# Scores and maxima of a tiled attention issued as four column tiles of 32 instead of one whole-array matmul

## Chip, cores and metric

One core of a Trainium2 chip runs the whole program. The metric is the device time of one execution in microseconds (us); of several runs the median is taken.

## What is computed

Sixteen images of 64 channels and 56 x 56 = 3136 pixels go through two layers. The first is attention inside windows of 7 x 7 pixels, with cosine scores, a bias table, three group norms and an MLP of width 256. The second is full attention over all 3136 pixels of an image, with 4 heads of 16 channels. Cut to what matters:

```python
# layer 1, of the layer-0 output x (n = 3136, heads = 4, d = 16)
qkv = jnp.einsum('oc,bchw->bohw', w_qkv, x)
q, k, v = jnp.split(qkv.reshape(b, 3 * c, n), 3, axis=1)
attn = jax.nn.softmax(jnp.einsum('bhdn,bhdm->bhnm', q, k) * scale, axis=-1)
out = jnp.einsum('bhnm,bhdm->bhdn', attn, v).reshape(b, c, h, w)
return jnp.einsum('oc,bchw->bohw', w_proj, out) + x
```

## The kernel before, in words

**Tiles of the second layer.** The keys and queries of a head lie in `k_stack` and `q_stack` in bf16, as six products' worth of three-piece splits stacked on 96 partitions (STACK), and three more rows (SHIFT) that subtract each query's maximum. The 3136 tokens are 25 tiles of 128 (TILES) on one side and 8 groups of 392 (GTOK) on the other. A stage is half of the queries (4 groups of 392) of one head, so an image has 8 stages and 8 x 25 = 200 quads. For each quad, that is for one tile of 128 keys:

- four steps `score` (function `score`, line 1285; matmul on line 1293): 99 rows, 128 keys as weights, 392 queries moving, out to one of three PSUM banks (SCORE_BANKS). Unit u first waits until the exponential of unit u - 3 is done.
- four exponentials on ScalarE (line 881), from PSUM to a ring of eight buffers in SBUF (`exps`, EXP_RING), in f32.
- one step `weigh` (line 1296; matmul on line 1304): four matmuls of `v_all` (128 rows, 32 columns, f32) with the four exponentials moving. Matmul j writes the PSUM partitions 32 j to 32 j + 31 of one bank, so the four lie side by side in the array as column tiles. An f32 matmul shows in the trace as two MATMULs and two LDWEIGHTS, so one `weigh` is eight of each.

The maxima are made ahead of a stage: a step `max` (line 1159) has two matmuls, 96 rows, 128 queries as weights, 392 keys moving, to the two banks of a slot, and VectorE reduces 784 columns to one (line 945). With 4 heads, 25 tiles and 4 pairs of groups there are 400 steps `max` per image, two per quad.

**Slots.** All steps of the first layer, the maxima, the shifts and the final projection use two PSUM slots in turn (RING_BANKS, banks 5 and 6, and 3 and 4). A step waits (function `free`) until the step two before it in the slots has been emptied by VectorE or ScalarE.

**Order.** The order of each engine's steps is written out by a planner when the program is built, with a fixed cost of each step and a fixed cost for going between steps that it lists as tiled and the others. The change leaves the planner's costs and lists alone, so every engine has its steps in the same order before and after. Image b + 1's first layer is woven into image b's attention. The first-layer steps on TensorE, per image: `qk` 4 (line 1173), `sum` 1 (line 1182, column tiles of 32), `spread` 4 (line 1190), `wscore` 16 (line 1200), `wval` 8 (line 1208), `wtrans` 16 (line 1218), `wpv` 8 (line 1229, column tiles of 32), `wproj` 8 (line 1236), `gn` 6 (line 1241), `mlp1` and `mlp2` 8 each (lines 1248, 1256), `gqk` 4 (line 1264), `gv` 3 (line 1273), and of the second layer `shift` 8 (line 1166) and `final` 4 (line 1282).

Of the kernel before, what the change touches and what calls it, by code (L numbers as in the profile page):

```python
# [10 lines left out]
GTOK = TOKENS // GROUPS  # L11
# [8 lines left out]
STACK = PIECES * D1  # L20
SHIFT = 3
# [5 lines left out]
SCORE_BANKS = 3  # L27
# [374 lines left out]
def attention_mlp_kernel(nc, x, qkv0, qkv0_b, logit_scale, table, rel_index, proj0, proj0_b, gn1_w, gn1_b,  # L402
# [10 lines left out]
    with ctx:  # L413
        def sb(name, shape, dt=f32):
            return ctx.enter_context(nc.sbuf_tensor(name, shape, dt))

        def sem(name):
            return ctx.enter_context(nc.semaphore(name))
# [42 lines left out]
        q_stack = sb("q_stack", [128, H1, PADTOK], bf16)  # L461
        k_stack = sb("k_stack", [128, H1, PADTOK], bf16)
# [20 lines left out]
        PS = ctx.enter_context(nc.psum_tensor("PS", [128, 8, 512], f32))  # L483
# [25 lines left out]
        s_scores, s_exps, s_pv_done, s_out_copied, s_out_stored = (sem(n) for n in (  # L509
            "scores", "exps", "pv_done", "out_copied", "out_stored"))  # L510
# [609 lines left out]
        def _(pe):  # L1120
            mm = nc.tensor.matmul
# [4 lines left out]
            for c in range(7):  # L1126
# [3 lines left out]
                   stop=True).then_inc(s_bias_product, 1)  # L1130
# [8 lines left out]
            def step(it, b, before):  # L1139
# [7 lines left out]

                if it.kind == "score":
                    score(it.i, b)
                elif it.kind == "weigh":  # L1150
                    weigh(it.i, b)
                elif it.kind == "max":
                    stage, tile, pair_ = it.i, it.j, it.k
# [2 lines left out]
                    free()  # L1156
                    for j in range(2):
                        chunk = 2 * pair_ + j
                        last = mm(PS[:, it.bank + j, 0:GTOK], q_stack[0:STACK, stage // 2, tile * 128:(tile + 1) * 128],  # L1159
                                  k_stack[0:STACK, stage // 2, chunk * GTOK:(chunk + 1) * GTOK], start=True, stop=True)  # L1160
                    last.then_inc(s_max_filled, 1)
                elif it.kind == "shift":
                    t0, t1 = STAGE_TILES[it.i % 2]
# [4 lines left out]
                elif it.kind == "qk":  # L1168
                    pe.wait_ge(s_x_by_windows, t * 8 + 2 * it.i + 2)
                    free()  # L1170
                    for j in range(2):
                        g = 2 * it.i + j
                        last = mm(PS[:, it.bank + j, 0:GTOK], w_qk0[:], x_w[:, g * GTOK:(g + 1) * GTOK],
                                  start=True, stop=True)
                    last.then_inc(s_qk_product, 1)
                elif it.kind == "sum":
                    pe.wait_ge(s_qk_squares, t * 4 + 4)
                    free()
                    for r in range(2):
                        for j in range(4):  # L1180
                            g = 4 * r + j
                            last = mm(PS[32 * j:32 * j + 32, it.bank, 0:GTOK], w_head_sum[:, r, :],
                                      tok_h[:, g * GTOK:(g + 1) * GTOK], start=(r == 0), stop=(r == 1))
                    last.then_inc(s_head_sums, 1)
                elif it.kind == "spread":
                    pe.wait_ge(s_norms_inverted, t + 1)
                    free()
                    for j in range(2):
                        g = 2 * it.i + j
                        last = mm(PS[:, it.bank + j, 0:GTOK], w_spread[:, g // 4, g % 4, :], tok_h[:, 0:GTOK],  # L1190
                                  start=True, stop=True)
                    last.then_inc(s_norms_spread, 1)
                elif it.kind == "wscore":
# [3 lines left out]
                    for i in range(4):  # L1197
                        w = 4 * half + i
                        q0, m = g * GTOK + w * WTOK, (64, WTOK)[w == 7]
                        last = mm(PS[64 * (w % 2):64 * (w % 2) + m, it.bank + i // 2, 0:GTOK],  # L1200
                                  tok_unit[0:CH + WTOK, q0:q0 + m], kmask[0:CH + WTOK, :, w * WTOK:(w + 1) * WTOK],
                                  start=True, stop=True)
                    last.then_inc(s_win_scores, 1)
                elif it.kind == "wval":
                    pe.wait_ge(s_x_twice, t * 8 + it.i + 1)
                    free()
                    for w in range(8):
                        last = mm(PS[0:2 * WTOK, it.bank, w * CH:(w + 1) * CH],  # L1208
                                  x_tw[:, w, :, :].rearrange("c a m -> c (a m)"), w_v0[:], start=True, stop=True)
                    last.then_inc(s_win_v, 1)  # L1210
                elif it.kind == "wtrans":
# [3 lines left out]
                    for p in range(2):  # L1215
                        for q in range(4):
                            c0 = (2 * half + p) * GTOK + q * 2 * WTOK
                            last = nc.tensor.transpose(PS[0:2 * WTOK, it.bank + p, q * 128:(q + 1) * 128],  # L1218
                                                       win_scores[:, c0:c0 + 2 * WTOK], ident_f32[:])
                    last.then_inc(s_win_transposed, 1)  # L1220
                elif it.kind == "wpv":
# [4 lines left out]
                    for w in range(8):  # L1226
                        for q in range(4):
                            c0 = q * 128 + 64 * (w % 2)
                            last = mm(PS[32 * q:32 * q + 32, it.bank, w * WTOK:(w + 1) * WTOK], win_v[:, w, q, :],
                                      win_probs_t[0:2 * WTOK, w // 2, c0:c0 + WTOK], start=True, stop=True)  # L1230
# [12 lines left out]
                elif it.kind == "mlp1":  # L1243
                    c = it.i
                    pe.wait_ge(s_mlp_in, t * 4 + c // 2 + 1)
                    free()
                    for e in range(2):
                        last = mm(PS[:, it.bank + e, 0:GTOK], w_1[:, 128 * e:128 * e + 128],  # L1248
                                  tok_qk[0:CH, c * GTOK:(c + 1) * GTOK], start=True, stop=True)
                    last.then_inc(s_mlp1, 1)  # L1250
                elif it.kind == "mlp2":
                    c = it.i
                    pe.wait_ge(s_hidden, t * 16 + 2 * c + 2)
                    free()
                    for e in range(2):
                        last = mm(PS[0:CH, it.bank, 0:GTOK], w_2[:, e, :], hidden[:, 2 * (c % 2) + e, :],  # L1256
                                  start=(e == 0), stop=(e == 1))
                    last.then_inc(s_mlp2, 1)
                elif it.kind == "gqk":
                    pe.wait_ge(s_z_ready, t * 4 + it.i + 1)  # L1260
                    free()
                    for j in range(2):
                        g = 2 * it.i + j
                        last = mm(PS[:, it.bank + j, 0:GTOK], w_qk1[:], z_w[:, g * GTOK:(g + 1) * GTOK],
                                  start=True, stop=True)
                    last.then_inc(s_gqk, 1)
                elif it.kind == "gv":
# [3 lines left out]
                    for tile in range(t0, t1):  # L1271
                        n_ = tile - t0
                        last = mm(PS[:, it.bank + n_ // 8, (n_ % 8) * CH:(n_ % 8 + 1) * CH],  # L1273
                                  z_w[:, tile * 128:(tile + 1) * 128], w_v1[:], start=True, stop=True)
                    last.then_inc(s_gv, 1)
                elif it.kind == "final":
# [3 lines left out]
                    for j in range(2):  # L1280
                        sl = slice((2 * k + j) * GTOK, (2 * k + j + 1) * GTOK)
                        last = mm(PS[0:CH, it.bank + j, 0:GTOK], w_p1[:], att[:, sl], start=True, stop=True)  # L1282
                    last.then_inc(s_final_proj, 1)

            def score(u, b):
                quad, j = u // 4, u % 4
                stage, kt = quad // TILES, quad % TILES
                h, c = stage // 2, 4 * (stage % 2) + j
                if kt == 0 and j == 0:
                    pe.wait_ge(s_shift_loaded, (b * STAGES + stage) * 48 + 48)  # L1290
                if u >= SCORE_BANKS:
                    pe.wait_ge(s_exps, b * UNITS + u - SCORE_BANKS + 1)
                mm(PS[:, u % SCORE_BANKS, 0:GTOK], k_stack[0:STACK + SHIFT, h, kt * 128:(kt + 1) * 128],  # L1293
                   q_stack[0:STACK + SHIFT, h, c * GTOK:(c + 1) * GTOK], start=True, stop=True).then_inc(s_scores, 1)

            def weigh(quad, b):
                stage, kt = quad // TILES, quad % TILES
# [14 lines left out]
            for it in PROLOGUE["PE"]:  # L1312
                step(it, -1, before)
            with pe.Fori(0, IMAGES - 1) as b:
                before = lead_in_emptied(b)
                for it in MORE["PE"]:
                    step(it, b, before)
            before = lead_in_emptied(IMAGES - 1)
            for it in LAST["PE"]:
                step(it, IMAGES - 1, before)  # L1320
# [57 lines left out]
```

## Time and profile before

| what | value |
|---|---|
| median of 3 runs | 10134.87 us |
| lowest and highest | 10125.32 and 10156.81 us |
| the profiled execution's own time | 10121.69 us |
| its span, first to last instruction | 10119.9 us |
| PE (matmuls) busy | 9685.7 us, 96% |
| VectorE busy | 7762.6 us, 77% |
| ScalarE busy | 6507.8 us, 64% |
| GpSimd busy | 974.3 us, 10% |
| mean granted TensorE clock | 0.968 of full speed |

PE stands for TensorE's matmuls and PEld for its weight loads. The busy time of PE takes each matmul from its start to the end of its latency, so matmuls that overlap are joined; how fast TensorE really goes is read from the distance between starts.

### The profile page before, as it was taken

How to read it: one execution, taken by the hardware profiler on the slowest of the kernel's cores; microseconds unless marked ns; L12 is line 12 of the kernel's file. 1: busy time of each engine (PE TensorE's matmuls, PEld its weight loads, DVE VectorE, ACT ScalarE, POOL GpSimd, SP SyncE). 2: the span in 40 equal slices, each digit the busy share in tenths (PEclk: the TensorE clock that was granted, in tenths of full speed). 3: DMA queues.
4: the chain of work that ended last, by engine and by line, in shares of the span. 5: the costliest groups of instructions: out<-in, count | busy, mean ns of one | idle time of the engine just before them, and what ended most of it. 6: DMA issues, size and time to landing. Idle time of an engine off the chain costs nothing.

```text
span 10119.9 us, 221389 instructions
## 1 busy us (share of the span) xinstructions
PE 9685.7 (96%) x69254; PEld 3807.6 (38%) x69254; DVE 7762.6 (77%) x10052; ACT 6507.8 (64%) x14066; POOL 974.3 (10%) x834
## 2 busy tenths in 40 slices
PE   5899999999999999999999999999999999999998
PEld 2333333333333343333433333333333433333332
DVE  4787777878778787787877778777787877878785
ACT  1466666666666667666666666666666666666676
POOL 3100101010010110101101010010101101011000
PEclk8799999999999999999999999999999999999999
DMA  0202011020110201102011020201102011020100
GB/s 24 35 7 39 10 21 27 6 41 8 22 26 5 42 8 27 21 8 40 7 29 20 9 39 7 37 13 21 27 6 41 9 24 24 5 43 8 25 16 16
DMA packets 109028, 213.92 MB, mean 21 GB/s; under 512 B 52854, under 2 KB 84534, under 8 KB 107706
## 3 DMA queue, kind: packets, MB, share of 16 engines
q1 hardware_dynamic: 107842, 198.78, 12.2%
q8 instruction: 663, 10.86, 0.5%
q14 instruction: 523, 4.28, 0.1%
HBM read 66.03 MB, written 41.47 MB: 11 GB/s over the span
## 4 chain that ended last, share of the span: by engine, by line
PE 83%; DVE 5%; DMA 4%; SPq 3%; issue 2%; ACT 2%; POOL 1%; DVEq 0%; ACTq 0%; POOLq 0%
PE PS L1304 23%; PE PS L1293 21%; PE PS L1159 20%; PE PS L1200 3%; DVE small L945 3%; PE PS L1218 2%; DMA x_in<-in_x 2%; PE PS L1208 2%; PE PS L1248 2%; PE PS L1256 2%; SPq L677 2%; ACT exps L881 1%; PE PS L1282 1%; PE PS L1273 1%; PE PS L1236 1%
## 5 line engine op out<-in xcount | busy, mean ns | idle before, releaser
L881 ACT ACTIVATE exps<-PS 128x392 f32<-128x392 f32 x12800 | 5591.0, 499 | 3029.7 <-PE PS L1293 2919.7
L945 DVE TENSOR_REDUCE small<-PS 128x1 f32<-128x784 f32 x6400 | 5942.3, 967 | 1172.7 <-PE PS L1159 1126.8
L1293 PE MATMUL PS<-q_stack,k_stack 99*128 99x392 bf16 x12800 | 3524.3, 336 | 31.8 <-ACT exps L881 19.3
L1159 PE MATMUL PS<-k_stack,q_stack 96*128 96x392 bf16 x12800 | 3186.0, 338 | 150.8 <-DVE small L945 79.6
L1304 PE MATMUL PS<-exps,v_all 128*32 128x392 f32 x25600 | 2823.2, 513 | 19.4 <-ACT exps L881 13.2
L1293 PEld LDWEIGHTS PS<-q_stack,k_stack 99*128 99x128 bf16 x12800 | 1200.0, 98 | 2418.8 <-ACT exps L881 1566.3
L1159 PEld LDWEIGHTS PS<-k_stack,q_stack 96*128 96x128 bf16 x12800 | 1049.3, 99 | 1728.4 <-DVE small L945 894.1
L1304 PEld LDWEIGHTS PS<-exps,v_all 128*32 128x32 f32 x25600 | 507.5, 108 | 998.5 <-issue 603.0
L780 POOL TENSOR_TENSOR win_scores<-win_scores,small 128x784 f32<-128x784 f32 x256 | 383.8, 1500 | 3351.2 <-DVE small L995 3351.2
L1200 PE MATMUL PS<-kmask,tok_unit 113*64 113x392 f32 (+1 forms) x2048 | 391.5, 506 | 7.5 <-DMA tok_unit<-in_query_ident 7.5
L983 DVE TENSOR_REDUCE small<-PS 128x16 f32<-128x784 f32 x256 | 249.2, 973 | 129.3 <-PE PS L1200 124.8
L838 ACT ACTIVATE win_probs_t<-PS 98x1024 f32<-98x1024 f32 x256 | 262.0, 1024 | 98.0 <-PE PS L1218 96.9
L1218 PE MATMUL PS<-ident_f,win_scores 128*98 128x128 f32 x2048 | 277.0, 280 | 18.7 <-DVE small L945 10.7
L986 DVE TENSOR_TENSOR win_scores<-PS,small 128x784 f32<-128x784 f32 x256 | 249.4, 974 | 31.5
L833 ACT ACTIVATE win_scores<-win_scores 128x784 f32<-128x784 f32 x256 | 221.0, 863 | 63.0 <-DVE win_scores L986 62.7
L793 POOL TENSOR_TENSOR att<-att,inv_sums 64x784 f32<-64x784 f32 x66 | 120.9, 1850 | 1459.0 <-DMA inv_sums<-scratch_rden 1459.0
L994 DVE TENSOR_REDUCE small<-win_scores 128x16 f32<-128x784 f32 x256 | 246.1, 961 | 14.1 <-ACT win_scores L833 10.9
L1218 PEld LDWEIGHTS PS<-ident_f,win_scores 128*98 128x98 f32 x2048 | 231.4, 130 | 66.3 <-DVE small L945 42.3
L1040 DVE SCALAR_TENSOR_TENSOR tok_h<-PS,vec,tok_h 64x392 f32<-64x392 f32 x128 | 79.1, 618 | 212.6 <-PE PS L1256 209.2
L1208 PE MATMUL PS<-w_v,x_tw 64*98 64x64 f32 x2048 | 210.6, 255 | 8.0 <-DVE win_scores L986 8.0
L930 DVE BATCH_NORM_STATS2 small<-tok_h 64x6 f32<-64x392 f32 x384 | 208.4, 556 | 9.8 <-ACT tok_h L848 1.1
L1208 PEld LDWEIGHTS PS<-w_v,x_tw 64*98 64x98 f32 x2048 | 192.9, 167 | 49.5 <-DVE win_scores L986 33.4
(102 smaller groups left out, 3938.5 us busy)
## 6 DMA issues: line engine op xcount, KB each, us to landing
q_stack<-tok_qk SPq DMA_DIRECT2D x320, 98.0 KB, 3.5
k_stack<-tok_qk SPq DMA_DIRECT2D x320, 98.0 KB, 4.2
kmask<-tok_unit SPq DMA_DIRECT2D x1024, 12.2 KB
scratch_att<-o_st SPq DMA_DIRECT2D x512, 26.0 KB
att<-scratch_att SPq DMA_DIRECT2D x33, 392.0 KB
z_half<-scratch_z SPq DMA_DIRECT2D x33, 392.0 KB, 11.1
inv_sums<-scratch_rden SPq DMA_DIRECT2D x132, 98.0 KB, 3.3
out<-inv_sums SPq DMA_DIRECT2D x33, 392.0 KB, 3.7
```

Source lines behind the costliest of these rows:

```text
L780: nc.gpsimd.tensor_tensor(S3, S3, rden[:, 16 * half:16 * half + 16].unsqueeze(2) .broadcast_to([128, 16, WTOK]), ALU.mult).then_inc(s_win_ ...
L838: nc.scalar.activation(win_probs_t[0:2 * WTOK, 2 * half:2 * half + 2, :], PS[0:2 * WTOK, it.bank:it.bank + 2, :], ACT.Copy)\
L881: nc.scalar.activation(exps(u), PS[:, u % SCORE_BANKS, 0:GTOK], ACT.Exp, scale=D1 ** -0.5).then_inc(s_exps, 1)
L945: nc.vector.tensor_reduce(max_parts[:, n_:n_ + 1], slot(), op=ALU.max, axis=AX.XY)\
L983: link(nc.vector.tensor_reduce(top, scores, op=ALU.max, axis=AX.X, negate=True))
L986: nc.vector.tensor_tensor(pair(win_scores, half).rearrange("p (a h m) -> p a h m", a=2, m=WTOK), scores, top.unsqueeze(3).broadcast_to([12 ...
L1159: last = mm(PS[:, it.bank + j, 0:GTOK], q_stack[0:STACK, stage // 2, tile * 128:(tile + 1) * 128], k_stack[0:STACK, stage // 2, chunk * GT ...
L1200: last = mm(PS[64 * (w % 2):64 * (w % 2) + m, it.bank + i // 2, 0:GTOK], tok_unit[0:CH + WTOK, q0:q0 + m], kmask[0:CH + WTOK, :, w * WTOK: ...
L1208: last = mm(PS[0:2 * WTOK, it.bank, w * CH:(w + 1) * CH], x_tw[:, w, :, :].rearrange("c a m -> c (a m)"), w_v0[:], start=True, stop=True)
L1218: last = nc.tensor.transpose(PS[0:2 * WTOK, it.bank + p, q * 128:(q + 1) * 128], win_scores[:, c0:c0 + 2 * WTOK], ident_f32[:])
L1293: mm(PS[:, u % SCORE_BANKS, 0:GTOK], k_stack[0:STACK + SHIFT, h, kt * 128:(kt + 1) * 128], q_stack[0:STACK + SHIFT, h, c * GTOK:(c + 1) * ...
L1304: last = mm(PS[32 * j:32 * j + 32, PV_BANK, 0:GTOK], v_all[:, stage // 2, kt, :], exps(4 * quad + j), start=(kt == 0), stop=(kt == TILES - 1))
```

## The change

Each matmul of `score` and of `max` is issued as four, each with 32 of the 128 weight columns and the same 392 moving columns, and each writing its own 32 PSUM partitions. The signal goes on the last of them. The waits stay where they were, ahead of the first.

```diff
                     for j in range(2):
                         chunk = 2 * pair_ + j
-                        last = mm(PS[:, it.bank + j, 0:GTOK], q_stack[0:STACK, stage // 2, tile * 128:(tile + 1) * 128],
-                                  k_stack[0:STACK, stage // 2, chunk * GTOK:(chunk + 1) * GTOK], start=True, stop=True)
+                        for q in range(4):
+                            last = mm(PS[32 * q:32 * q + 32, it.bank + j, 0:GTOK],
+                                      q_stack[0:STACK, stage // 2, tile * 128 + 32 * q:tile * 128 + 32 * q + 32],
+                                      k_stack[0:STACK, stage // 2, chunk * GTOK:(chunk + 1) * GTOK],
+                                      start=True, stop=True)
                     last.then_inc(s_max_filled, 1)
...
-                mm(PS[:, u % SCORE_BANKS, 0:GTOK], k_stack[0:STACK + SHIFT, h, kt * 128:(kt + 1) * 128],
-                   q_stack[0:STACK + SHIFT, h, c * GTOK:(c + 1) * GTOK], start=True, stop=True).then_inc(s_scores, 1)
+                for q in range(4):
+                    last = mm(PS[32 * q:32 * q + 32, u % SCORE_BANKS, 0:GTOK],
+                              k_stack[0:STACK + SHIFT, h, kt * 128 + 32 * q:kt * 128 + 32 * q + 32],
+                              q_stack[0:STACK + SHIFT, h, c * GTOK:(c + 1) * GTOK], start=True, stop=True)
+                last.then_inc(s_scores, 1)
```

## Rows read from the trace of the kernel before

**Rows 1.** The page's busy time of each engine, share of the span, instructions.
```profile
PE 9685.7 (96%) x69254; PEld 3807.6 (38%) x69254; DVE 7762.6 (77%) x10052; ACT 6507.8 (64%) x14066; POOL 974.3 (10%) x834
```

**Rows 2.** The page's chain that ended last, shares by engine.
```profile
PE 83%; DVE 5%; DMA 4%; SPq 3%; issue 2%; ACT 2%; POOL 1%; DVEq 0%; ACTq 0%; POOLq 0%
```

**Rows 3.** The page's costliest groups: busy us, mean ns of one, idle before, releaser.
```profile
L881 ACT ACTIVATE exps<-PS 128x392 f32<-128x392 f32 x12800 | 5591.0, 499 | 3029.7 <-PE PS L1293 2919.7
L945 DVE TENSOR_REDUCE small<-PS 128x1 f32<-128x784 f32 x6400 | 5942.3, 967 | 1172.7 <-PE PS L1159 1126.8
L1293 PE MATMUL PS<-q_stack,k_stack 99*128 99x392 bf16 x12800 | 3524.3, 336 | 31.8 <-ACT exps L881 19.3
L1159 PE MATMUL PS<-k_stack,q_stack 96*128 96x392 bf16 x12800 | 3186.0, 338 | 150.8 <-DVE small L945 79.6
L1304 PE MATMUL PS<-exps,v_all 128*32 128x392 f32 x25600 | 2823.2, 513 | 19.4 <-ACT exps L881 13.2
```

**Rows 4.** Timeline of PE, attention alone: start us, us, instructions merged.
```profile
4001.97 0.87 PE L1304 MATMUL PS<-exps,v_all 128*32 128x392 f32 x8
4002.77 0.34 PE L1293 MATMUL PS<-q_stack,k_stack 99*128 99x392 bf16 x1
4002.94 0.50 PE L1159 MATMUL PS<-k_stack,q_stack 96*128 96x392 bf16 x2
...
4003.95 0.33 PE L1293 MATMUL PS<-q_stack,k_stack 99*128 99x392 bf16 x1
4004.20 0.87 PE L1304 MATMUL PS<-exps,v_all 128*32 128x392 f32 x8
```

**Rows 5.** Timeline of DVE in the same stretch.
```profile
4003.48 1.86 DVE L945 TENSOR_REDUCE small<-PS 128x1 f32<-128x784 f32 x2 [0.38 <-PE PS L1159]
```

**Rows 6.** Timeline of ACT in the same stretch.
```profile
4003.14 1.86 ACT L881 ACTIVATE exps<-PS 128x392 f32<-128x392 f32 x4 [0.38 <-PE PS L1293]
```

**Rows 7.** Timeline of PE where the step `sum` stands, and what follows it.
```profile
4118.06 1.52 PE L1182 MATMUL PS<-tok_h,w_head_sum 128*32 128x392 f32 x16
4119.51 0.34 PE L1293 MATMUL PS<-q_stack,k_stack 99*128 99x392 bf16 x1
```

**Rows 8.** Timeline of PE where `weigh` follows `wpv`.
```profile
4173.94 0.90 PE L1229 MATMUL PS<-win_probs_t,win_v 98*32 98x49 f32 x64
4174.66 0.85 PE L1304 MATMUL PS<-exps,v_all 128*32 128x392 f32 x8
4175.44 0.51 PE L1159 MATMUL PS<-k_stack,q_stack 96*128 96x392 bf16 x2
```

**Rows 9.** Timeline of PE around a step `wtrans`.
```profile
5003.82 0.33 PE L1293 MATMUL PS<-q_stack,k_stack 99*128 99x392 bf16 x1
5003.99 1.04 PE L1218 MATMUL PS<-ident_f,win_scores 128*98 128x128 f32 x8
5004.86 0.66 PE L1293 MATMUL PS<-q_stack,k_stack 99*128 99x392 bf16 x3
```

**Rows 10.** Timeline of PE, the one `weigh` of 4200 to 4222 next to another shape.
```profile
4210.04 0.87 PE L1304 MATMUL PS<-exps,v_all 128*32 128x392 f32 x8
4210.83 1.54 PE L1200 MATMUL PS<-kmask,tok_unit 113*64 113x392 f32 x8
```

**Rows 11.** Timeline of the weight loads in the stretch of rows 4.
```profile
4002.78 0.27 PEld L1159 LDWEIGHTS PS<-k_stack,q_stack 96*128 96x128 bf16 x2
```

**Rows 12.** Waits of the weight loads: us in total, times, longest us.
```profile
PEld PS L1293 <- ACT exps L881: 1566.3, 3149, 1.3
PEld PS L1159 <- DVE small L945: 894.1, 1710, 1.3
```

**Rows 13.** The page's DMA queue of instruction fetches: packets, MB, share of 16 engines.
```profile
q8 instruction: 663, 10.86, 0.5%
```

**Rows 14.** Windows: length, busy us of PE, PEld, DVE, ACT, POOL, clock, DMA share, GB/s.
```profile
4200.00:4450.00 250.00, 246.00 (x2031) 99.53 (x2028) 208.37 (x270) 167.49 (x364) 22.60 (x18) 1.00 0.03 7
4700.00:4750.00 50.00, 46.07 (x208) 15.19 (x205) 27.03 (x38) 22.30 (x47) 12.34 (x11) 0.76 0.27 42
```

## The prediction

> **What bounds the kernel now.** I read the page's busy times first [rows 1]: PE is busy 96% of the span, VectorE 77%, ScalarE 64%. A busy PE joins latencies, so I asked the chain next [rows 2]: 83% of it is PE. DMA and its queue, 7%, stand mostly where images meet. The groups [rows 3] say what PE does: 12,800 scores, 12,800 matmuls of maxima, and 25,600 MATMULs of the weighted sums, eight to a step, so 3200 steps `weigh`. Then I looked at how far apart matmuls start [rows 4]. In a stretch with attention alone, a cycle of one quad goes from `weigh` at 4001.97 to `weigh` at 4004.20, 2.23 us. Score and maximum start 0.17 us apart, which is 392 columns at the rate that eight of them keep up. The last score starts at 4003.95 and the `weigh` behind it only at 4004.20, 0.25 us later and not 0.17: 0.08 to 0.10 us in which the array is given nothing. `weigh` then holds 0.80 us until the next score starts (4001.97 to 4002.77).
>
> How much of 0.80 us is work? The step `sum` has the same form with sixteen MATMULs, four passes of four tiles, and lasts 1.45 us [rows 7]. The difference of two passes is 0.65 us, so a pass is 0.33 us, and `weigh` is 0.66 us of streaming and 0.14 us of something else. Where `weigh` follows `wpv`, itself in column tiles of 32, it starts 0.72 us after 64 matmuls that stream 49 columns each at 0.04 us per four; there is no hole on that side, and it lasts 0.78 us [rows 8]. So the hole belongs to the change of shape, about 0.10 us on each side, and the last 0.02 to 0.04 us are the first weight load, which nothing hid, and the stagger of four starts. It is not a matter of rows: `wpv` has 98 and `weigh` 128 and they join without a hole; a score (99 rows, 128 columns) and `wtrans` (128 rows, 98 columns) join without one too, 0.17 us apart [rows 9].
>
> **The change, part by part.** It removes the change of shape on both sides of nearly every `weigh`. It adds three matmuls and three weight loads to each of 25,600. It moves no step and adds no wait.
>
> *Removed.* A `weigh` with its two sides costs 2.23 - 8 x 0.167 = 0.90 us now, and two passes would cost 0.66: 0.24 us, or 0.12 us a side. There are 6400 sides. From 4200 to 4222 us, where the first layer is woven in, there are nine whole steps `weigh`, and one of their 18 sides is next to another shape [rows 10]. I take 95%: 6080 x 0.12 = 730 us. The 128 steps `wpv` and 16 steps `sum` lose their two holes as well: 144 x 2 x 0.10 = 29 us.
>
> *Added holes.* `wtrans` joins a score without a hole today [rows 9] and would not any more; `spread` has the same whole-array shape. (16 + 4) x 16 = 320 steps, two sides, 0.12 us: 77 us back. All other first-layer steps already have a shape of their own, so they keep their holes; each now also waits for four staggered starts, 0.02 us a side on some 1100 steps: 45 us back.
>
> *The column tiles themselves.* No row shows four bf16 tiles at once. The nearest rows are the f32 passes: four tiles, 392 columns, 0.33 us [rows 7], and the single bf16 matmul, 0.167 us [rows 4]. These are the two ends. I take the lower, for this reason: `wtrans` streams eight times 128 f32 columns through the undivided array in 0.87 us [rows 9], 0.85 ns a column, and four f32 tiles side by side take 0.33 us for 392, also 0.84 ns a column. Four streams at once cost f32 nothing. A bf16 column has half the bytes and half the time of an f32 one, so four bf16 streams ask for as many bytes per ns as the f32 tiles get. The opposite end is 25,600 x 0.163 = 4170 us. A gain below 0.167 us is excluded: each tile must still take in 392 columns.
>
> *Issue.* `wpv` gives 64 loads and 64 matmuls in 0.72 us [rows 8], 0.045 us for four pairs. Four pairs per 0.167 us is a quarter of that rate, so this hides behind streaming; if the cover went, it would be 0.045 us a group. Instruction fetches: 153,600 more instructions beside 221,389 would make some 460 packets more than 663, and 0.35% more DMA share [rows 13]; I cost them at nothing.
>
> *Weight loads.* Two loads of 128 bf16 columns run in 0.27 us under matmuls that start every 0.17 us [rows 11], and `wpv` loads 32 columns and streams 49 in 0.045 us per four, so loads for a tile run under that tile's own matmul. The ends are nothing and the 0.03 us by which the first load of `weigh` shows, times 25,600, 770 us. I take nothing in a running stream and 0.02 us after a wait. PE's loads stand 4859 times on ScalarE or VectorE [rows 12]; about half of these already pay at a changed shape, so 2400 x 0.02 = 50 us back.
>
> The Trainium skill, "TensorEngine Tiling (Array Packing)", section "Restrictions and Gotchas", says that column tiling turns off the fast weight load, and "TensorE: Matmul & The Clock Gate", section "The mechanism", says that a load overlaps a running matmul only when its row group differs. Taken with that page's load time of columns / 1.2 ns, four loads of 32 would be 107 ns in the open per group, an estimate of 2.7 ms in all. The trace disagrees as far as it goes [rows 8, 11], for f32 tiles and for whole bf16 loads.
>
> *Sum.* 730 + 29 - 77 - 45 - 50 = 587 us off PE.
>
> **What of it reaches the end.** In the pure stretch VectorE reduces twice in 1.86 us and idles 0.38 [rows 5], ScalarE does four exponentials in 1.86 us and idles 0.38 [rows 6]. With PE's cycle at 2.00 us both would idle about 0.14, so PE still sets the pace, closely. In the mixed stretch PE is busy 246 of 250 us, VectorE 208 and ScalarE 167 [rows 14]: more room. At the seam of two images, as in 4700 to 4750, VectorE is busy 27 of 50 us and the granted clock is 0.76: there PE waits for chains over DMA, and less drain time is worth nothing. PE is 83% of the chain; of its 96% that is seven eighths. I take 0.86 of 587: 505 us. Late next are VectorE's reductions, which free the slots, and ScalarE's exponentials, three banks behind the scores; a wait on either stands on the first of the four loads, and the next three loads, four matmuls and all later steps of PE queue behind it. From the profiled execution's 10,122 us this makes 9617; the median of the runs is 13 us above it, 0.1%, so against it I say 9630. Differences under 0.3%, about 30 us, can't be told from no change.
>
> **The rivals.**
> *Four bf16 streams go at the f32 tiles' pace* (the side of slower). Place: each of 25,600 groups, 0.33 for 0.167 us. Price 4170 us, less 587: about 13,700 us. It decides from 587 / 25,600 = 0.023 us more per group. For it: no row has four bf16 streams. Against: the bytes, as above. Chance 0.07.
> *The loads show.* Up to 0.03 us per group, 770 us: between 9630 and 10,300 us. For it: the load of `weigh` shows after a hole. Against: `wpv`. Chance 0.08, half of it slower. The two rules of the Trainium skill cited above point this way.
> *Others take PE's place.* VectorE and ScalarE have 0.38 us per cycle, but jitter eats it, and half of 587 turns into waits on lines 945 and 881: 9830 us. For it: 4859 waits already. Against: both engines idle a sixth of the pure cycle and more elsewhere. Chance 0.08.
> *The change doesn't do what it says*: 96 and 99 rows are another shape than 128, the holes stay, and a group costs its stagger of 0.02 us: 10,122 + 510 = 10,630 us. Against: 98 and 128 rows join without a hole [rows 8]. Chance 0.03.
>
> **How the numbers follow.** The forecast case has 0.74; its own range is 9450 (all of 730 us gained with little given back) to 9800. The range up to 9950 takes in the third rival and the mild half of the second, and leaves out the other two: 9450 to 9950. Faster 0.82, same 0.03, slower 0.15 (0.07 + 0.05 + 0.03).
>
> **What the profile after would show.** Lines 1293 and 1159 with 51,200 MATMULs each, 99*32 and 96*32. In the pure stretch a cycle of about 2.00 us, the score 0.17 us ahead of `weigh` and groups of four every 0.17 us. `weigh` lasting 0.66 to 0.70 us from start to start. A new hole of about 0.10 us at `wtrans`. VectorE near 81% and ScalarE near 68%. I am wrong if groups start further apart than 0.19 us, if the hole before `weigh` is still there, or if waits on lines 945 and 881 grow by more than 200 us.

## The result, and the profile after

| | before | after |
|---|---|---|
| median of 4 runs | 10145.84 us | 9773.05 us |
| lowest and highest | 10125.32 and 10175.44 us | 9745.64 and 9798.49 us |
| the profiled execution's own time | 10121.69 us | 9798.49 us |

The ratio is 0.963, with a 95% interval of 0.9593 to 0.9667: 3.7% faster, 373 us by the medians. The forecast was 9630 us, a gain of 505 us, in a range of 9450 to 9950. Direction and mechanism are as forecast; the gain is three quarters of what was said. The time lies 143 us above the forecast and 57 us below the 9830 us of the third rival.

The page of the changed kernel: busy time, the DMA queue of instruction fetches, the chain that ended last, and the costliest groups (idle and releaser at the end).

```profile
PE 9247.3 (94%) x146054; PEld 4488.6 (46%) x146054; DVE 7697.9 (79%) x10052; ACT 6526.0 (67%) x14066; POOL 975.9 (10%) x834
...
q8 instruction: 1256, 20.58, 0.9%
...
PE 74%; DVE 11%; issue 5%; DMA 4%; SPq 3%; ACT 2%; POOL 1%; DVEq 0%; ACTq 0%; POOLq 0%
...
L945 DVE TENSOR_REDUCE small<-PS 128x1 f32<-128x784 f32 x6400 | 5882.0, 967 | 891.5 <-PE PS L1160 822.0
L1297 PE MATMUL PS<-q_stack,k_stack 99*32 99x392 bf16 x51200 | 3687.5, 336 | 66.7 <-issue 36.8
L1160 PE MATMUL PS<-k_stack,q_stack 96*32 96x392 bf16 x51200 | 3311.8, 337 | 170.5 <-DVE small L945 88.5
L1310 PE MATMUL PS<-exps,v_all 128*32 128x392 f32 x25600 | 2764.9, 502 | 22.4 <-ACT exps L881 13.7
```

Against [rows 2] the chain tells the story: PE fell from 83% to 74% and VectorE rose from 5% to 11%. The "issue" share, time for which the profile shows no wait, went from 2% to 5%. TensorE gave up part of its place on the chain.

The timeline of PE in a stretch with attention alone, to be laid beside [rows 4]:

```profile
3905.53 0.83 PE L1310 MATMUL PS<-exps,v_all 128*32 128x392 f32 x8
3906.19 0.34 PE L1297 MATMUL PS<-q_stack,k_stack 99*32 99x392 bf16 x4
3906.36 0.51 PE L1160 MATMUL PS<-k_stack,q_stack 96*32 96x392 bf16 x8
3906.69 0.51 PE L1297 MATMUL PS<-q_stack,k_stack 99*32 99x392 bf16 x8
3907.03 0.51 PE L1160 MATMUL PS<-k_stack,q_stack 96*32 96x392 bf16 x8
3907.36 0.34 PE L1297 MATMUL PS<-q_stack,k_stack 99*32 99x392 bf16 x4
3907.53 0.83 PE L1310 MATMUL PS<-exps,v_all 128*32 128x392 f32 x8
```

Each part of the forecast cycle is there. From `weigh` to `weigh` it is 2.00 us, where it was 2.23. The score starts 0.17 us ahead of `weigh` (3907.36 to 3907.53), where it was 0.25, and `weigh` gives way to the next score after 0.66 us, where it was 0.80. Two groups of four bf16 tiles take 0.33 to 0.34 us (3906.36 to 3906.69), what two whole matmuls took: four bf16 streams at once run at full pace.

VectorE in the same stretch, and in a mixed one:

```profile
3906.92 3.85 DVE L945 TENSOR_REDUCE small<-PS 128x1 f32<-128x784 f32 x4 [0.19 <-PE PS L1160]
```
```profile
4096.97 6.37 DVE L945 TENSOR_REDUCE small<-PS 128x1 f32<-128x784 f32 x7
4104.11 0.97 DVE L983 TENSOR_REDUCE small<-PS 128x16 f32<-128x784 f32 x1 [0.77 <-PE PS L1203]
```

In the pure stretch VectorE now runs four reductions, two cycles, in one piece and idles 0.19 us in 4.0, where two reductions stood between idle times of 0.38 [rows 5]. In the mixed stretch it runs seven reductions in one piece, 6.37 us, and then idles 0.77 waiting for a first-layer step. My reading is that TensorE gets its slots back only at VectorE's pace in the full part, and that VectorE can't make up for the empty part.

The new hole at `wtrans`, in the timeline of PE:

```profile
4062.94 0.51 PE L1297 MATMUL PS<-q_stack,k_stack 99*32 99x392 bf16 x8
4063.38 1.08 PE L1221 MATMUL PS<-ident_f,win_scores 128*98 128x128 f32 x8
4064.39 0.35 PE L1160 MATMUL PS<-k_stack,q_stack 96*32 96x392 bf16 x4
```

Two groups end 0.33 us after 4062.94, and `wtrans` starts 0.44 us after it: 0.11 us of hole. It holds 1.01 us, where it held 0.87 [rows 9].

The waits of the weight loads, to be laid beside [rows 12]:

```profile
PEld PS L1160 <- DVE small L945: 1089.4, 2962, 1.2
PEld PS L1297 <- ACT exps L881: 869.8, 2969, 0.7
```

The waits on VectorE grew from 1710 to 2962 times. Those on ScalarE went from 1566 to 870 us in about as many. This view has to be read with care: PEld's idle time runs beside matmuls. Before, it also holds the holes: the first load of the `weigh` at 4004.20 starts together with its matmul, 0.25 us after the last score, though that score streams for 0.17. So it is no sum of lost time.

For that I added up PE's records another way: over the whole trace the distance from one group's start to the next, less what the group streams at full clock (0.163 us for 392 bf16 columns, 0.327 for an f32 pass). What is left over at a change of shape, up to 0.097 us and the stagger, is a hole; what is left beyond it there, or beyond 0.014 us elsewhere, is a wait. Half-clock stretches (1.2 instead of 2.4 GHz) count as waits too. The 0.097 is a cap that I set, so that a hole can't come out larger. That it isn't smaller is in the trace: of the 7910 changes of shape before and the 2426 after that fell at full clock, none was under 0.092 us. In us:

| kernel | changes of shape | holes | waits |
|---|---|---|---|
| before | 8117 | 848 | 1105 |
| after | 2534 | 259 | 1358 |

The holes lost 589 us. The waits took 253 us back. The difference, 336 us, is the 323 us between the two profiled executions, within 13. The column of waits is not all waiting; its parts stand with the experiment half_reduce.

### The profile page after: what moved, and what is told of

The parts are those of the page before. It is cut to its first block, busy times and chain, and to the rows that moved or that the text cites. A ratio compares the mean times of both kernels' runs of the same rounds, so it can differ in the third digit from the quotient of the medians.

```text
span 9796.7 us, 374989 instructions
## 1 busy us (share of the span) xinstructions
PE 9247.3 (94%) x146054; PEld 4488.6 (46%) x146054; DVE 7697.9 (79%) x10052; ACT 6526.0 (67%) x14066; POOL 975.9 (10%) x834
## 4 chain that ended last, share of the span: by engine, by line
PE 74%; DVE 11%; issue 5%; DMA 4%; SPq 3%; ACT 2%; POOL 1%; DVEq 0%; ACTq 0%; POOLq 0%
PE PS L1160 18%; PE PS L1310 18%; PE PS L1297 18%; DVE small L945 8%; PE PS L1203 4%; PE PS L1221 3%; DMA x_in<-in_x 2%; PE PS L1251 2%; PE PS L1259 2%; PE PS L1211 2%; SPq L677 2%; ACT exps L881 1%; PE PS L1285 1%; PE PS L1267 1%; PE PS L1239 1%
## 5 line engine op out<-in xcount | busy, mean ns | idle before, releaser
L945 DVE TENSOR_REDUCE small<-PS 128x1 f32<-128x784 f32 x6400 | 5882.0, 967 | 891.5 <-PE PS L1160 822.0
L1297 PE MATMUL PS<-q_stack,k_stack 99*32 99x392 bf16 x51200 | 3687.5, 336 | 66.7 <-issue 36.8
L1160 PE MATMUL PS<-k_stack,q_stack 96*32 96x392 bf16 x51200 | 3311.8, 337 | 170.5 <-DVE small L945 88.5
L1310 PE MATMUL PS<-exps,v_all 128*32 128x392 f32 x25600 | 2764.9, 502 | 22.4 <-ACT exps L881 13.7
L1297 PEld LDWEIGHTS PS<-q_stack,k_stack 99*32 99x32 bf16 x51200 | 1411.6, 96 | 1736.8 <-ACT exps L881 869.8
L1160 PEld LDWEIGHTS PS<-k_stack,q_stack 96*32 96x32 bf16 x51200 | 1176.3, 96 | 1901.8 <-DVE small L945 1089.4
L1310 PEld LDWEIGHTS PS<-exps,v_all 128*32 128x32 f32 x25600 | 785.6, 112 | 368.0 <-ACT exps L881 70.5
L1203 PEld LDWEIGHTS PS<-kmask,tok_unit 113*64 113x64 f32 (+1 forms) x2048 | 124.7, 135 | 222.9 <-issue 114.1
L1251 PE MATMUL PS<-tok_qk,w 64*128 64x392 f32 x512 | 211.0, 552 | 8.0 <-DVE small L945 5.5
```

What stands on the lines that cost most here:

```text
L945: nc.vector.tensor_reduce(max_parts[:, n_:n_ + 1], slot(), op=ALU.max, axis=AX.XY)\
L1160: last = mm(PS[32 * q:32 * q + 32, it.bank + j, 0:GTOK], q_stack[0:STACK, stage // 2, tile * 128 + 32 * q:tile * 128 + 32 * q + 32], k_sta ...
L1297: last = mm(PS[32 * q:32 * q + 32, u % SCORE_BANKS, 0:GTOK], k_stack[0:STACK + SHIFT, h, kt * 128 + 32 * q:kt * 128 + 32 * q + 32], q_stac ...
L1310: last = mm(PS[32 * j:32 * j + 32, PV_BANK, 0:GTOK], v_all[:, stage // 2, kt, :], exps(4 * quad + j), start=(kt == 0), stop=(kt == TILES - 1))
```

## The experiments

**Question.** Two theories say where the missing part went. Theory 1: TensorE gave up what was forecast, and VectorE's slots took part of it back as waits. Theory 2: the column tiles cost TensorE something, by their instructions, stagger or loads.

**scores_only.** The maxima stay whole. The cut is against the changed kernel.

```diff
-                        for q in range(4):
-                            last = mm(PS[32 * q:32 * q + 32, it.bank + j, 0:GTOK], ...
+                        last = mm(PS[:, it.bank + j, 0:GTOK], q_stack[0:STACK, stage // 2, tile * 128:(tile + 1) * 128],
+                                  k_stack[0:STACK, stage // 2, chunk * GTOK:(chunk + 1) * GTOK], start=True, stop=True)
```

> Half of the change: the scores go as four column tiles, the maxima stay whole. Counted through the order of TensorE's steps, changes of tile shape go from 8117 in the kernel before to about 13,130 (to 2534 with the whole change), since maxima now stand as a foreign shape between scores and weighted sums. Theory, a change of shape costs 0.10 us: 5000 more, some 500 us on TensorE, nearly all of it on the path, since TensorE is then busier and the others idler: 10,550 to 10,650 us. Rival, the gain of the whole change came from something in the column tiles themselves (loads or streaming of bf16 tiles) and not from the shape: half of the gain, about 9950 us.

Measured, in two executions: 10,420.9 us, ratio to the kernel before 1.0287 (1.0252 to 1.0322), 293 us slower. The number was missed, by both theories. Half of the change is worse than none, as theory 1 says, but by 293 us and not 500. The timeline of PE shows the hole at its full price:

```profile
3905.63 0.34 PE L1294 MATMUL PS<-q_stack,k_stack 99*32 99x392 bf16 x4
3905.90 0.50 PE L1159 MATMUL PS<-k_stack,q_stack 96*128 96x392 bf16 x2
3906.34 0.52 PE L1294 MATMUL PS<-q_stack,k_stack 99*32 99x392 bf16 x8
```

From score to maximum it is 0.27 us, and 0.44 us from two maxima to the next score, where streaming alone is 0.17 and 0.33: 0.10 us each. Summed as above, the holes are 1338 us, 490 more than before for 5016 more changes, 0.098 us each. Of the 12,742 changes at full clock none was under 0.092 us. The waits fell from 1105 to 897, 208 less. So waits give way when TensorE gets slower, as they fill up when it gets faster. 490 - 208 = 282, against 277 us between the two profiled executions and 293 by the medians.

**half_reduce_before and half_reduce_after.** Both kernels with VectorE relieved: a reduction takes 392 columns, not 784.

```diff
-                    nc.vector.tensor_reduce(max_parts[:, n_:n_ + 1], slot(), op=ALU.max, axis=AX.XY)\
+                    nc.vector.tensor_reduce(max_parts[:, n_:n_ + 1], PS[:, it.bank, 0:GTOK], op=ALU.max, axis=AX.X)\
```

> The kernel before, with VectorE's maxima taken over 392 of the 784 columns of a slot, so half of the keys are left out of the maximum. Reduction from 0.97 to about 0.56 us; VectorE from 77% to some 50% busy. TensorE's waits on line 945 go, the holes at changed shapes stay. Both theories: 9850 to 10,000 us. It is the base for the next one.

> The changed kernel with the same lighter maxima (392 of 784 columns; half of the keys are left out of the maximum). Theory 1, TensorE gave up its 587 us as forecast and VectorE's slots took back the missing part as waits: with VectorE light the gain against half_reduce_before is 500 us or more (5% and up), and the waits of line 1160 on line 945 are small. Theory 2, the column tiles cost TensorE what is missing (four times the instructions, staggered starts, results that come later): the gain stays near the 372 us, 3.7%, of the full kernels.

Measured: 9989.2 us (ratio to the kernel before 0.9856, 0.9834 to 0.9879) and 9445.5 us (0.9327, 0.9309 to 0.9344). Between the two it is 544 us, 5.4%, past the 500 of theory 1. Theory 2 said 372 and falls as the account of what is missing. The chain and the waits of half_reduce_after:

```profile
PE 8965.7 (95%) x146054; PEld 4606.4 (49%) x146054; DVE 5386.2 (57%) x10052; ACT 6476.2 (69%) x14066; POOL 975.6 (10%) x834
...
PE 83%; DMA 4%; ACT 4%; SPq 3%; issue 2%; DVE 2%; POOL 1%; ACTq 0%; DVEq 0%; POOLq 0%
```
```profile
PEld PS L1297 <- ACT exps L881: 963.3, 2994, 1.6
...
PEld PS L1160 <- DVE small L945: 278.4, 1047, 0.8
```

TensorE is 83% of the chain again, and the waits of line 1160 on VectorE fell from 1089 to 278 us. By the sum of distances: holes 847 to 260 us, waits 1004 to 1012. The holes go as in the full kernels (587 us).

That the waits come out level hides several movements. Here are the same distances, split further (this sum sorts some 100 to 140 us more into waits in each kernel, so read the differences), in us of the profiled executions:

| | before | after | half_reduce_before | half_reduce_after |
|---|---|---|---|---|
| holes | 846 | 258 | 845 | 257 |
| second pass of `weigh` late | 93 | 23 | 94 | 23 |
| matmuls at half clock, the longer streaming | 238 | 304 | 269 | 188 |
| idle ahead of maxima | 301 | 431 | 126 | 133 |
| idle ahead of scores | 164 | 207 | 213 | 301 |
| idle ahead of all other steps | 449 | 525 | 432 | 478 |
| all else, mostly streaming | 7980 | 7999 | 7982 | 8002 |

- *A third part of the hole.* Before, the second pass of `weigh` started 0.356 us after the first (median), after the change 0.333. That is the first load that nothing hid, 70 us in all. It goes with the change of shape, so TensorE gave up 658 us and not 589.
- *The cost of the column tiles.* The last row grew by 19 and 20 us, below 1 ns for each of 25,600 groups. This is what is left of theory 2.
- *VectorE's slots.* With the full reductions the idle time ahead of maxima grew by 130 us, with the light ones by 7. This is theory 1, shown. It is not the whole of the waits.
- *ScalarE.* With VectorE light the idle time ahead of scores, which wait for exponentials, grew by 88 us. With VectorE out of the way ScalarE took its place.
- *The clock.* TensorE's matmuls lost 66 us more to the half clock after the change, and 81 us less in the light pair; the mean granted clock went from 0.968 to 0.959, and from 0.965 to 0.971. In the profiled executions this makes 147 us of the 257 by which the two gains, 323 and 580 us, differ. The medians differ by less (373 and 544), and so do the clocks of the other executions (0.962 to 0.965 after). Whether the waits on VectorE brought the clock down was not tested.

So the 544 us are near the forecast 587 in part by luck: TensorE gave up more, ScalarE took some back, and the clock helped.

**scores_only_half.** It asks whether the miss of scores_only was the waits or the price.

```diff
 (scores_only with the tensor_reduce of half_reduce_before)
```

> scores_only (scores in column tiles, maxima whole) with VectorE's maxima over 392 of 784 columns, so half of the keys are left out of the maximum. scores_only cost 293 us over the kernel before, where 5016 more changes of shape at 0.10 us would be 500. Theory 1, a change of shape costs its 0.10 us and the waits for VectorE's slots give way by the rest: with VectorE light there is less to give way, and the cost over half_reduce_before (9989 us) is 400 us or more. Theory 2, a change between these shapes costs only 0.06 us: it stays at 293 us.

Measured: 10,365.5 us, 376 us above half_reduce_before (ratios to the kernel before 1.0211, 1.0171 to 1.0252, and 0.9856, 0.9834 to 0.9879). The two were not measured side by side; by the ratios it is 360 us, give or take some 47. It is short of the 400 that was asked for, and above 293 by little more than the spread, so the times alone hardly decide. The holes do: they are 490 us more again, the waits 878 against 1004, 126 less. The price of a change of shape is the same 0.10 us; how much of it reaches the end seems to differ, in the direction of theory 1.

**more_tiles.** The change carried on to those first-layer matmuls with 98 or more rows and 64 columns.

```diff
-                    mm(PS[0:CH, it.bank, 0:GTOK], w_p0[:], tok_qk[:, g * GTOK:(g + 1) * GTOK], start=True, stop=True)\
-                        .then_inc(s_win_proj, 1)
+                    for c0 in (0, 32):
+                        last = mm(PS[c0:c0 + 32, it.bank, 0:GTOK], w_p0[:, c0:c0 + 32],
+                                  tok_qk[:, g * GTOK:(g + 1) * GTOK], start=True, stop=True)
+                    last.then_inc(s_win_proj, 1)
...
```

(`mlp2` in the same way, and `wscore` with 32 and 32, or 32 and 17, columns.)

> The changed kernel, and also the first layer's wscore, wproj and mlp2 matmuls (which have 98 or more rows and 64 columns) as column tiles of 32. Changes of shape fall from 2534 to about 1660, 870 fewer at 0.11 us: 95 us off TensorE. Theory 1 (waits take part of it back): 50 to 70 us faster than the changed kernel, 9700 to 9720. Theory 2 (each column tile costs): these steps get more matmuls, so no gain or a loss.

Measured: 9689.3 us, ratio to the kernel before 0.9566 (0.9548 to 0.9583), where the changed kernel has 0.963 (0.9593 to 0.9667). By the ratios that is some 65 us faster than the changed kernel, give or take 41, and 84 us by the medians, for 89 us fewer holes. Theory 2, no gain or a loss, falls here too. That the waits took part of it back isn't shown: by the finer sum waits and half clock together stood at 1474 us in the changed kernel and 1466 here. With replan_found below it is the fastest of the kernels here that compute everything. Its chain is PE 68%, VectorE 15%: a further step that frees TensorE hands more to VectorE.

**replan, replan_more and replan_found.** The planner that orders the steps is told of the shapes. In replan this is on the changed kernel, in replan_more on more_tiles, and replan_found has other settings of the same planner.

```diff
-SWITCH, TILED, URGENT = 9, ("weigh", "sum", "wscore", "wpv"), 7
+SWITCH, URGENT = 10, 7
+SHAPE = {**dict.fromkeys(("weigh", "sum", "wpv", "score", "max"), 1), **dict.fromkeys(("wscore", "wproj", "mlp2", "shift"), 2),
+         **dict.fromkeys(("qk", "mlp1", "gqk", "gv", "wval"), 3), **dict.fromkeys(("gn", "final"), 4)}
...
-            duration += SWITCH * (self.tiled != (kind in TILED))
-            self.tiled = kind in TILED
+            duration += SWITCH * (self.tiled != SHAPE.get(kind, 0))
+            self.tiled = SHAPE.get(kind, 0)
```

> The changed kernel with the planner told of the shapes: weighted sums, scores, maxima, sum and wpv are one shape, the first layer's others have theirs, and each change costs 0.10 us; all engines' orders come out anew. The order of the changed kernel was laid out for holes that are gone. Theory 1, the waits for VectorE's slots come from buffers and the mean load, but partly from an order that no longer fits: 20 to 100 us faster than the changed kernel's 9773. Rival, the slots alone set them: no difference beyond 30 us, or a chance loss.

> more_tiles with the planner told of its shapes. Against more_tiles (9689 us) theory 1 expects 20 to 100 us less, the rival no difference beyond 30 us.

> more_tiles with another order of steps. The two replanned orders (10,409 and 10,278 us) had stretches in which neither the maxima nor the exponentials were supplied; this order was picked out of some 300 that the planner writes when its settings are varied (maxima may lag further, overdue first-layer steps come sooner, score cost 20 for 17). Theory 1, the order decides how much of the saved time turns into waits: 9550 to 9680 us, faster than more_tiles (9689). Rival, the waits come from the two slots whatever the order, and any new order loses by chance: 9700 us or more.

Measured: 10,408.9 us (ratio 1.0263, 1.0228 to 1.0299), 10,278.2 us (1.0132, 1.0097 to 1.0167) and 9702.9 us (0.9571, 0.9551 to 0.9591). All three expectations of theory 1 were missed. Two windows of replan where two images meet, 50 us each (busy us of PE, PEld, DVE, ACT, POOL, clock, DMA share, GB/s):

```profile
4100.00:4150.00 50.00, 38.27 (x509) 19.89 (x511) 15.40 (x19) 29.17 (x65) 8.06 (x7) 0.83 0.71 97
4150.00:4200.00 50.00, 43.41 (x633) 16.51 (x625) 45.88 (x59) 18.81 (x42) 4.23 (x3) 0.79 0.08 20
```

First VectorE has 15 us of work in 50 while the DMA engines are 71% busy, and right after it 46 while ScalarE has 19: the order feeds one and then the other. TensorE's clock is granted at 0.83 and 0.79 meanwhile. Holes fell to 223 us, but waits rose to 2019 us. Part of that is the clock: its mean is 0.918 over the span, against 0.959, and the finer sum has 548 us of longer streaming at half clock, against 304. So an order can throw away all of the gain and more. replan_found balances the engines again (waits 1379 us) and is the same as more_tiles to within the intervals. Theory 1 had said 9680 us or less for it, and the rival 9700 or more, so the number is the rival's. That the order could bring back more of the 253 us is not shown; none of three new orders did.

## Why the prediction was right, and where it was off

- *The hole at a change of shape, 0.10 us.* Right. 5583 fewer changes took 589 us of holes away, and scores_only added 490 us for 5016.
- *The rest of the 0.24 us per `weigh`* (first load and stagger). Right in the pure stretch, where 0.90 us became 0.66, and over the whole: holes and late second passes fell by 658 us, where 730 + 29 - 77 = 682 was forecast.
- *95% of 6400 sides, and 320 steps that get holes.* Right as a count: 6080 + 288 - 640 gives 5728 fewer, the trace has 5583. The sample behind the 95% was miscounted: from 4200 to 4222 us seven steps `weigh` are whole, not nine, so it was one side of 14.
- *Four bf16 streams, priced at the lower end.* Right: groups start 0.17 us apart. The rival of 13,700 us, that they go at the f32 tiles' pace, did not happen.
- *Weight loads and issue hidden.* Right in the stream. The Trainium skill ("TensorE: Matmul & The Clock Gate", section "The mechanism") has, in its list of what overlaps, a load overlap a running matmul only where the row group differs (above the list it also names a background weight buffer as a target). The trace doesn't agree with the list: here a load and the matmul before it share their rows (96 or 99, from the first on), and four loads per 0.17 us stayed hidden. Instruction fetches rose by 593 packets, not 460, to 0.9% of the DMA engines. I ran nothing to test what they cost.
- *587 us off TensorE.* Somewhat low: 658 us less 19 is some 640, in the profiled executions. The 95 us given back for stagger and for loads after a wait were too much: the runs show 19 or 20 us of such costs. That 589 us of holes come so near to 587 is luck.
- *0.86 of it reaches the end.* This is the step that failed. It was 373 of 587, 0.64, and less of the 640 that TensorE really gave up. I took PE's share of the chain, seven eighths of its busy time, for the share that would still be on it afterwards. A chain gives the share at the old speed; it doesn't tell how close the next engine is. I did look at that, but by means: in the pure stretch at one cycle, where the idle 0.38 us fell to 0.19 in two cycles, and in the mixed stretch at VectorE's 208 of 250 us. What counts is bunches: first-layer steps and maxima share the two slots and VectorE, which is full for 6.37 us and then empty for 0.77. The cover for a late slot is one slot, not the mean. Shown is that the waits ahead of maxima go when VectorE is light. That they gather in the mixed stretch is not: of the 250 us by which idle time grew in the finer sum, without the late second passes, 196 lie within 4 us of a first-layer step, 78%, and so does 77% of the time at full clock. The pure stretch lost as much per microsecond as the mixed one. The third rival (half of 587, 293 us, turned into waits, 9830 us) had the right mechanism and nearly the price: the waits grew by 253 us. I gave it a chance of 0.08. The result stands nearer to it than to the forecast; that it also lies in the forecast case's own range, 9450 to 9800, is owed to the width of that range. In the chances, half of the second rival's 0.08 is 0.04, where 0.05 was used.
- *The clock* is no term of the sum. The half clock at the seams was seen [rows 14], but that its share could grow was not considered. It took 66 us more than before in the profiled executions.
- *The signs of being wrong.* Groups start 0.17 us apart and the hole before `weigh` is gone, as forecast. The waits on lines 945 and 881 in the view of [rows 12] fell, from 2460 to 1959 us; but that view can't serve as the sign it was meant to be, for idle time on TensorE did grow. VectorE is 79% busy and ScalarE 67%, against 81 and 68.

Mean busy times hardly show that TensorE shares its place now. Windows of the changed kernel in its mixed part, and of more_tiles in the same part:

```profile
4100.00:4350.00 250.00, 243.12 (x4196) 117.48 (x4188) 216.91 (x285) 177.94 (x383) 22.62 (x18) 1.00 0.03 8
```
```profile
4100.00:4350.00 250.00, 242.36 (x4155) 120.43 (x4151) 211.47 (x286) 180.03 (x387) 19.37 (x16) 1.00 0.03 7
```

PE's busy time went from 246 of 250 us [rows 14] to 243 and 242. At 97% it still looks like the only bound.

## What to carry to other kernels

Where matmuls of two array shapes alternate, read the distance from start to start on both sides; if the short steps can be cut to the shape of the others at the same streaming rate, cut all of the neighbours, since cutting half of them adds changes of shape. Judge how much of a saving reaches the end by the room that the next engines have when their work bunches, not by the bound engine's share of the chain. Relieving that next engine in both kernels (a lighter operation that leaves the rest alone) comes nearer to the full gain, and tells a cost of the change from a wait behind it. Then look at what else moved, here the waits on ScalarE and the clock. A bad order can cost more than such a change brings (636 us for replan), and a more truthful cost table doesn't by itself give a better order.

## What the runs showed of the hardware that was not expected

Four column tiles stream 392 bf16 columns each in the 0.167 us of one whole matmul, with four loads of 32 columns hidden under them; the f32 rows could only suggest this. Once the shape is the same, the first load of `weigh` is hidden too: 0.80 us with its exit hole became 0.66, two passes of 0.33 and nothing else. A change of shape never cost less than 0.092 us in some 23,000 of them at full clock, in three traces. In scores_only, tiles of 32 with 99 rows and whole matmuls with 96 rows, both in bf16, change over at the same 0.10 us as f32 and bf16 steps did; and in the changed kernel f32 and bf16 steps of one shape join without a hole. The price goes with the shape and not with the type.
